# First feed-forward base product as three rounded passes, weights split at the end of the attention

## The reference

```python
xf = layernorm(x)                                  # 1024 rows of 512
logits = xf @ W_router.T                           # 8 experts
topk_p, topk_i = top_k(softmax(logits), 2)         # two are kept, renormalised into combine
h = einsum('nd,erd->ner', xf, A_stack) * combine   # rank 16 for each expert
lora_out = einsum('ner,eor->no', h, B_stack) * 2.0
out = (xf @ W_base.T + b_base) + lora_out          # W_base 512 x 512
x = x + tanh(g_ffn[0]) * out
```

## Time and profile before

| | us |
|---|---|
| median of 3 runs (lowest, highest) | 1709.88 (1707.79, 1710.16) |
| the profiled execution | 1705.91 |
| its span | 1703.8 |
| PE busy | 1611.8 (95%) |
| DVE busy | 949.7 (56%) |
| ACT busy | 741.6 (44%) |
| POOL busy | 348.0 (20%) |

### The profile page before, as it was taken

One profiled execution on the slowest core, in us unless ns is written; L12 is line 12 of the kernel. 1 busy time (PEld: TensorE's weight loads), 2 busy tenths in 40 slices (PEclk: granted clock), 3 DMA queues, 4 the chain that ended last, 5 costly groups with the idle time before them and its releaser, 6 DMA issues.

```text
span 1703.8 us, 26093 instructions
## 1 busy us (share of the span) xinstructions
PE 1611.8 (95%) x9028; PEld 1282.9 (75%) x9028; DVE 949.7 (56%) x2491; ACT 741.6 (44%) x2174; POOL 348.0 (20%) x242
## 2 busy tenths in 40 slices
PE   9999999999999999999998999999999899889875
PEld 7888888888888888888765869687876697445545
DVE  5652524525345253452577756667575757566687
ACT  4542443424434244342423544536363231776642
POOL 3210212102121021210024000000003433232352
PEclk9999999999999999999999999999999999999988
DMA  5111101111011110110430000000016112000001
GB/s 182 53 41 45 45 28 52 40 46 43 28 52 40 40 50 28 52 40 25 137 163 23 14 13 0 9 3 0 1 38 195 41 53 82 6 14 13 1 1 49
DMA packets 34133, 76.04 MB, mean 45 GB/s; under 512 B 5536, under 2 KB 18336, under 8 KB 31904
## 3 DMA queue, kind: packets, MB, share of 16 engines
q1 hardware_dynamic: 34080, 75.36, 13.1%
HBM read 73.25 MB, written 2.10 MB: 44 GB/s over the span
## 4 chain that ended last, share of the span: by engine, by line
PE 68%; DVE 15%; ACT 8%; issue 4%; POOL 2%; DVEq 2%; DMA 0%; POOLq 0%; ACTq 0%; SPq 0%
PE banks L963 14%; PE banks L973 10%; PE banks L1060 10%; PE banks L1163 9%; PE banks L1267 5%; ACT p L872 3%; PE banks L1239 3%; PE banks L1031 3%; DVE sA L1588 3%; PE banks L1046 2%; ACT sA L669 2%; PE banks L1376 2%; PE banks L1038 1%; DVE sA L1600 1%; PE banks L1143 1%
## 5 line engine op out<-in xcount | busy, mean ns | idle before, releaser
L1611 DVE TENSOR_TENSOR x_res<-banks,x_res 128x512 f32<-128x512 f32 x120 | 82.8, 691 | 207.7 <-PE banks L1060 207.3
L963 PE MATMUL banks<-cT,w_k 128*128 128x512 f32 x720 | 179.8, 398 | 0.0
L973 PE MATMUL banks<-w_v,cT 128*128 128x512 f32 x768 | 179.8, 392 | 0.0
L963 PE MATMUL banks<-xT,w_q 128*128 128x512 f32 x720 | 175.3, 396 | 0.0
L1060 PE MATMUL banks<-w_o,atT 128*128 128x512 f32 x720 | 170.0, 392 | 2.2 <-DVE x_res L1611 2.0
L669 ACT ACTIVATE sA<-sA,nmA 128x128 f32<-128x128 f32 x256 | 99.4, 392 | 166.6 <-DVE nmA L1588 165.6
L973 PEld LDWEIGHTS banks<-w_v,cT 128*128 128x128 f32 x768 | 142.7, 188 | 29.0
L1060 PEld LDWEIGHTS banks<-w_o,atT 128*128 128x128 f32 x720 | 133.6, 188 | 31.7 <-DVE x_res L1611 2.9
L963 PEld LDWEIGHTS banks<-xT,w_q 128*128 128x128 f32 x720 | 131.9, 188 | 25.4
L963 PEld LDWEIGHTS banks<-cT,w_k 128*128 128x128 f32 x720 | 130.8, 188 | 25.2
L1595 DVE TENSOR_SCALAR rsA<-smA 128x4 f32<-128x4 f32 x64 | 15.7, 245 | 185.6 <-ACT sA L669 185.6
(11 more groups left out here) (244 smaller groups left out, 3255.3 us busy)
## 6 DMA issues: line engine op xcount, KB each, us to landing
w_raw_k<-in_w0k SPq DMA_DIRECT2D x16, 512.0 KB, 3.3
w_raw_v<-in_w0v SPq DMA_DIRECT2D x8, 1024.0 KB, 7.3
w_raw_q<-in_w0q SPq DMA_DIRECT2D x15, 512.0 KB, 3.3
w_raw_o<-in_w0o SPq DMA_DIRECT2D x15, 512.0 KB, 3.3
cTp<-in_ctxT SPq DMA_DIRECT2D x12, 512.0 KB, 3.8
wq_raw<-in_wq SPq DMA_DIRECT2D x1, 3072.0 KB, 11.2
wo<-in_wo SPq DMA_DIRECT2D x1, 3072.0 KB, 20.9
kT<-in_ctxT SPq DMA_DIRECT2D x4, 512.0 KB, 6.9
```

What stands on the lines that cost most here:

```text
L963: mm = pe.matmul(dst, w[l][:, c, h * P:(h + 1) * P], t[r][:, c, half * 512:(half + 1) * 512], start=n == 0, stop=n == 3 * DC - 1)
L973: mm = pe.matmul(dst, cT[l][:, c, b * P:(b + 1) * P], wv_[r][:, c, :], start=n == 0, stop=n == 3 * DC - 1)
L1611: dve.tensor_tensor(x_res[:, b, :], bank(6 + b % 2), x_res[:, b, :], ALU.add).then_inc(S("o_added"), 1)
```

## The change

Feed-forward 0 gets the form of feed-forward 1. Its base product takes three passes over parts. L0F is added to PARTS, so xnT is stored both whole and as parts. The high part of the base weights (f0p[0]) is copied by ScalarE in the last head pair, the low part (f0p[1]) computed by GpSimd after its last split. The low part takes the place of the raw weights. wv1_raw moves to where wo1 goes, so wo1's load waits until the low parts of wk1 and wv1 are made. The counts of the shared semaphores wf_hi and wf_lo move up by one.

```diff
-PARTS = {L1X: 0, L1F: 1, L2X: 2, L2F: 3}
+PARTS = {L0F: 0, L1X: 1, L1F: 2, L2X: 3, L2F: 4}
...
+        f0_high = sb(ctx_a, "f0base_0", [P, DC, D], F32R)
...
+        ffn["f0"]["base"] = sb(ctx_g, "f0base", [P, DC, D])
+        ctx_g.close()
+        ctx_g = ExitStack()
+        f0p = [f0_high, sb(ctx_g, "f0base_1", [P, DC, D], F32R)]
...
             for t, n in ((wk1_raw, "wk1"), (wv1_raw, "wv1")):
                 sp.dma_start(t[:], A[n]).then_inc(S("wkv1_ld"), 16)
+            sp.wait_ge(S("wkv1_lo"), 2)
             sp.dma_start(wo1[:], A["wo1"]).then_inc(S("wo1_ld"), 16)
...
             split("q", NHP - 1)
+            pool.wait_ge(S("wf_hi"), 1)
+            for c in range(DC):
+                e = pool.tensor_tensor(f0p[1][:, c, :], ffn["f0"]["base"][:, c, :], f0p[0][:, c, :].bitcast(F32), ALU.subtract)
+            e.then_inc(S("wf_lo"), 1)
...
                 store_at(p, 0)
                 store_pT(p, 1)
+                act.wait_ge(S("ffn_ld"), 64)
+                act.activation(f0p[0][:], ffn["f0"]["base"][:], ACT.Copy).then_inc(S("wf_hi"), 1)
                 store_at(p, 1)
...
-                        if second:
-                            wait_parts(L, i, j)
+                        wait_parts(L, i, j)
                         for c in range(DC):
-                            if second:
-                                for n, (l, r) in enumerate(PASSES):
-                                    pe.matmul(bank(4 + j), xnTp[l][:, c, t], f1p[r][:, c, :], start=c == 0 and n == 0, stop=False)
-                            else:
-                                pe.matmul(bank(4 + j), xnT[:, c, t], w["base"][:, c, :], start=c == 0, stop=False)
+                            for n, (l, r) in enumerate(PASSES):
+                                pe.matmul(bank(4 + j), xnTp[l][:, c, t], parts[r][:, c, :], start=c == 0 and n == 0, stop=False)
...
-                if second:
-                    pe.wait_ge(S("wf_lo"), 1)
+                pe.wait_ge(S("wf_lo"), second + 1)
...
+            for j in range(2):
+                part_lo(L0F, 0, j)
             ffn_dve(L0F, 4, 2.0)
```

More of the change, by code:

```diff
@@ L141, in build @@
         ctx_g = ExitStack()
-        ffn["f0"] = dict(base=sb(ctx_g, "f0base", [P, DC, D]), ra=sb(ctx_g, "f0ra", [P, DC, NE + NE * RANK]),
-                         up=sb(ctx_g, "f0up", [P, D]))
+        sb(ctx_g, "f0_pad", [P, 2 * DC * PT2])
+        ffn["f0"] = dict(ra=sb(ctx_g, "f0ra", [P, DC, NE + NE * RANK]), up=sb(ctx_g, "f0up", [P, D]))
         ctx_g.close()
@@ L213, in build @@
         wv1 = [sb(ctx_1, f"wv1_{l}", [P, DC, KV1 * HD1], F32R) for l in range(2)]
+        ctx_x = ExitStack()
+        wv1_raw = sb(ctx_x, "wv1_raw", [P, DC, KV1 * HD1])
+        ctx_x.close()
         wo1 = sb(ctx_1, "wo1", [P, NCH * KV1, D])
@@ L222, in build @@
         wk1_raw = sb(ctx_x, "wk1_raw", [P, DC, KV1 * HD1])
-        wv1_raw = sb(ctx_x, "wv1_raw", [P, DC, KV1 * HD1])
         ctx_x.close()
@@ L531, in _ @@
             pairs_ahead(pool, x1_pool)
-            rest(f1p, ffn["f1"]["base"], "wf")
+            rest(f1p, ffn["f1"]["base"], "wf", 2)
             def x2_end():
@@ L549, in x2_pool @@
                     context_rest(NPAIR + i + 2)
-            pairs_split(pool, x2_pool, lambda: rest(w2, zp2, "wf", 2), nothing, nothing)
+            pairs_split(pool, x2_pool, lambda: rest(w2, zp2, "wf", 3), nothing, nothing)
             rsqrt(NPAIR * (L2F - 1) + 1)
@@ L593, in x3_pool @@
                         c = u - G3
-                        pool.wait_ge(S("wf_hi"), c + 3)
+                        pool.wait_ge(S("wf_hi"), c + 4)
                         e = pool.tensor_tensor(wg3p[1][:, c, :], wg3[:, c, :], wg3p[0][:, c, :].bitcast(F32), ALU.subtract)
@@ L1167, in ffn_pe @@
             def ffn_pe(L, f):
-                w, second = ffn[f], int(L == L1F)
+                w, second, parts = ffn[f], int(L == L1F), f1p if L == L1F else f0p
                 def body(i, last):
@@ L1479, in _ @@
             pairs_ahead(pe, x2_pe)
-            pe.wait_ge(S("wf_lo"), 2)
+            pe.wait_ge(S("wf_lo"), 3)
             pairs_ahead(pe, f2_pe)
@@ L1491, in _ @@
             f3_turn(0)
-            pe.wait_ge(S("wf_lo"), 4)
+            pe.wait_ge(S("wf_lo"), 5)
             f3_gate_up(0)
```

## The result

| | before | after |
|---|---|---|
| median of 19 runs each (lowest, highest), us | 1709.32 (1705.90, 1711.21) | 1712.55 (1709.63, 1714.25) |
| the profiled execution | 1705.91 | 1710.08 |
| its span | 1703.8 | 1708.0 |

The ratio is 1.0023, with a 95% interval of 1.0016 to 1.0030, so the changed kernel is slower, by about the 0.2% under which the prediction speaks of no change. The medians differ by 3.2 us (0.19%). TensorE's base product did get cheaper, 24 rows in 5.64 us in place of 16 in 6.86, but the time is lost elsewhere.

A forecast was written before the change was run, and what follows sets the result against it. The chain was taken as mixed around the changed stage, TensorE holding 68% of it over the span and VectorE 15%. +2.4 at the attention's end and +0.45 in the stage gave +2.9: 1709.88 + 2.9 = 1712.8 us, range 1708.4 to 1716.2.

The forecast's parts named there:

- Attention end: VectorE's sums there delayed by GpSimd's new subtractions, plus possible low clock: 2.4 us lost.
- The turns: At the attention's end GpSimd's subtractions and VectorE's begin_sums alternate by instruction: 2.0 us on the chain, bounds 0 and 5.1.
- the low clock: After TensorE's idle at the attention's end, twelve matmuls at 1.2 GHz would cost another 0.85 us, if it comes.
- The stage: First feed-forward: -0.45 + 0.9 = +0.45 us in all, bounds 0 and +0.9.
- T0: First pair's transpose of hs, first work after the base product: forecast 885.0, before 886.13, gain 1.1 us.
- T1: Second pair's transpose of hs: forecast 895.7, before 897.66, gain 1.9 us in all.
- T2: Third pair's transpose of hs, held by ScalarE's wq copy and GpSimd's wq1 split: forecast 915.9, gain 0.45 us.
- Pair 3: Last pair of the stage: later statistics and low clock lose 0.45 to 1.3 us, 0.9 taken.
- What was priced at nothing: ScalarE's high-part copy, before which it idles 5.35 us, and wo1's later load, some 40 us of slack: price 0.
- (a): Attention's end: GpSimd keeps its turn for all four subtractions, 5.1 us slip, 1715.4 us; chance 0.15.
- (b): Feed-forward: cheaper products count, 1704.8 us with all four gains, 1708.0 with the first two pairs' only; chance 0.08.
- (c): Attention's end: collision costs nothing but the stage's gain is eaten, +0.45, 1710.3 us; chance 0.17.

The follow-up runs named there:

- e5: Changed kernel with GpSimd's split of wq1 in pieces of 256 columns; median 1709.76 us, ratio 1.0006 to the kernel before.
- e3: Changed kernel's preparation alone, with the base product direct in float32 as before; median 1712.62 us, ratio 1.0020 to the kernel before.
- e8: Kernel before with GpSimd's split of wq1 in pieces of 512 columns; median 1708.36 us, ratio 0.9998 to the kernel before.
- e2: Changed kernel with f0base's low part made by one GpSimd instruction of 128x2048, not four of 128x512; median 1715.50 us, ratio 1.0045.
- e1: Changed kernel with low-part subtractions of 8 columns, not 512, TensorE reading the high part instead of the low; median 1709.11 us, ratio 1.0002.
- e4: Kernel before with GpSimd's split of wq1 in pieces of 256 columns, not 1536; median 1705.61 us, ratio 0.9981 to the kernel before.
- e6: Changed kernel with f0base's low part made after GpSimd's first rsqrt; median 1713.08 us, ratio 1.0027 to the kernel before.

## Why the prediction came out right, and where two errors met

The forecast was slower by 2.9 us on the execution's own time; the medians differ by 3.2, the profiled executions by 4.2, of which 0.6 arose before any edit. The mechanism was the one named. Two sizes were off, in opposite directions, so the closeness of the sum (2.9 said; 3.51 from begin_sum to end, 3.2 between the medians) is in part luck.

**Attention end: said 2.4, measured 3.58.** The turns were right in kind, and in size as far as it can be told (+2.0; e5 2.05 with the low clock of before, 1.2 for e3 against e8; the subtraction 1.72 with a turn, said 1.15 and 0.55). One of the readings behind them was loose: beside L2057 GpSimd had pieces of 128x256, 0.72 us alone, and then of 128x512, 1.27 alone, not of 0.6. The term that was mis-sized is the low clock: 0.85 if it came, of which I took half. It came, behind 2.01 us of idle (said 2.5), and cost 1.3 us on the 24 matmuls there (7.31, before 6.00), for which end_sum waited 1.04 and 0.92; against e5 it is 1.53. It does not come each time. e3 had its 6.8 us of low clock in one stretch from 860.0, under VectorE's sums: its begin_sums start at the same distances as e5's, which had 3.4. e5 had no second stretch, though TensorE idled 2.23 us, and e2 none behind 3.07. So idle time alone doesn't decide it, and how often it comes in the other runs of the changed kernel stays open.

**The stage: said +0.45, measured -0.07.** T0 gained 1.26 (said 1.1), T1 2.16 (1.9), T2 0.62 (0.45). ScalarE's copy of wq came 3.28 behind T1 (said 3.27), TensorE's idle grew to 9.35 (said 9), and from T2 to the statistics it was 6.0 (said 6 to 6.8). Pair 3 then lost 0.55 where I took 0.9. The base product took 5.64 from first to hs, said 5.59. The 216 ns that the Trainium skill ("TensorE: Matmul & The Clock Gate", Back-to-back issue gap) gives between matmuls of 512 columns would make it 5.2. The trace again shows more, 235.

**What was priced at nothing cost nothing that can be seen.** e1 shows this for ScalarE's copy of the high part, the second copies of xnT and the wo1 wait together. ScalarE still idles 3.56 us behind the new copy. The load of wo1 was issued late and landed in 11.2 us, against 20.9 in the earlier trace rows. Two rows of the timeline, and the DMA issue:

```profile
856.37 0.60 ACT L693 ACTIVATE atT<-banks 128x512 fp32r<-128x512 f32 x1 [3.56 <-PE banks L1062]
...
935.58 0.33 SPq L412 DMA_DIRECT2D wo<-in_wo  x1
```

```profile
wo<-in_wo SPq DMA_DIRECT2D x1, 3072.0 KB, 11.2
```

**The rivals.** (a), the turn kept, is refuted by the rows of four pieces and shown in e2 for one. (b), the products count, is refuted by e1: with a free preparation they bring 0.17 us. Its premise, that the split of wq1 hides them, is e4's and e5's finding, and once that is shortened they bring 0.6, since behind T2 the stage is VectorE's. (c), a collision at no cost, is refuted by e1 against after (3.63 us to the copy).

Still open is which place for the subtractions would cost nothing. Three were tried: two met a VectorE chain that TensorE was waiting for, and in the third TensorE waited for the subtractions themselves. e6 with its wait moved behind the router product was not tried, nor pieces of 256 in the place of the changed kernel.

## What to carry to other kernels

Before giving an idle engine a piece of work, look at what the engine beside it does there with operands from SBUF, and at whether anybody waits for it: a GpSimd subtraction of 128x512 costs each VectorE operation of that kind that it meets 0.7 to 1.1 us, and the same piece in another place only meets other ones. Where small VectorE operations on the chain run beside long GpSimd ones, cut the GpSimd pieces first; here 1536 to 256 columns was worth 3.75 us, more than the products it was meant to uncover, while 512 columns showed nothing in the time. A cheaper product pays only until the next engine is the later one: follow the gain pair by pair to the end of the stage.

## What the runs showed of the hardware that I had not expected

- What is held is a matter of one instruction, whatever its size: tw on 128x2 columns took 3.19 us beside a piece of 1536 columns, 0.97 beside 512 and 0.43 beside 256. The mask operations of 128x128 took 1.22 to 1.36 beside 512 columns and 0.82 beside 256, alone 0.29.
- Shorter pieces cost GpSimd a quarter more at most: 10.17 us for three of 1536, 11.22 for nine of 512 (e8), 12.74 for eighteen of 256, the turns included.
- What goes with the granted clock is as large as the effects under study: 1.53 us at the end of the attention, 1.34 there between e4 and e8 with the same code, and up to 4 behind the last copy of xnT between kernels whose code is the same there.
